# One graph-network layer on one core: staging, counts, first offsets, bias and pads of the setup rearranged

## The reference

```
h   = concat(x[src], x[dst], edge_attr) @ W + b
h   = (h - mean(h)) / sqrt(var(h) + 1e-5) * gamma + beta
out = segment_sum(relu(h), src, 6250)
y   = layernorm(x + out)
```

## Time and profile before

| | us |
|---|---|
| median of 3 runs | 1229.41 |
| profiled execution | 1233.39 |
| its span | 1231.5 |
| TensorE (PE) busy | 986.8 |
| VectorE (DVE) busy | 928.1 |
| POOL busy (784 scatters 766.6) | 782.5 |
| ScalarE (ACT) busy | 711.7 |
| mean granted TensorE clock | 0.947 |

### The profile page before, as it was taken

The page is one execution under the profiler, slowest core; times in us unless marked ns, Lnnn a source line. Parts: engine busy times, 40 slices in busy tenths (PEclk is TensorE's granted clock), DMA queues, the critical chain, the costliest instruction groups (busy, mean ns, idle before and its releaser), DMA issues.

```text
span 1231.5 us, 36181 instructions
## 1 busy us (share of the span) xinstructions
PE 986.8 (80%) x9913; PEld 867.3 (70%) x9914; DVE 928.1 (75%) x2787; ACT 711.7 (58%) x2814; POOL 782.5 (64%) x810
## 2 busy tenths in 40 slices
PE   6789977988888887888787778888887878577784
PEld 5667767887777787777777777777777777566651
DVE  7675447987777777777777777777777777689987
ACT  3324455765655656655555656566556556467765
POOL 0067676777777777777777777777777777700030
PEclk9789888999999989999999999999899999799998
DMA  8677567766666666666766766676666665333303
GB/s 215 180 236 220 175 203 217 239 194 197 195 191 193 191 192 199 199 185 192 194 189 188 199 188 197 188 204 197 192 187 200 194 183 150 113 106 92 99 19 104
DMA packets 192458, 221.57 MB, mean 180 GB/s; under 512 B 51350, under 2 KB 141802, under 8 KB 192272
## 3 DMA queue, kind: packets, MB, share of 16 engines
q1 hardware_dynamic: 166236, 163.92, 48.5%
q0 software_dynamic: 25088, 54.64, 12.0%
q10 hardware_dynamic: 948, 0.79, 0.3%
HBM read 147.95 MB, written 71.30 MB: 178 GB/s over the span
## 4 chain that ended last, share of the span: by engine, by line
DMA 19%; issue 16%; POOL 16%; DVE 16%; PE 15%; ACT 12%; DVEq 3%; SPq 3%; POOLq 0%; ACTq 0%
POOL rows L685 16%; DMA rows<-p,pos_idx 15%; ACT late L1189 6%; DVE late L1586 5%; PE bank L964 3%; DVE room L1570 3%; DVEq L495 2%; ACT turn L1151 2%; PE bank L918 2%; PE bank L858 2%; PE bank L942 1%; DMA tabB<-room 1%; DVE room L1562 1%; PE bank L871 1%; PE bank L869 1%
## 5 line engine op out<-in xcount | busy, mean ns | idle before, releaser
L685 POOL DMA_INDIRECT rows<-p,pos_idx x784 | 766.6, 978 | 309.8 <-issue 275.4
L1189 ACT ACTIVATE late<-room 128x128 f32<-128x128 f32 x864 | 256.1, 298 | 288.7 <-DVE room L1570 286.0
L964 PE MATMUL bank<-wc,turn 128*128 128x128 f32 x1552 | 238.8, 301 | 10.6 <-ACT turn L1151 7.0
L1586 DVE SCALAR_TENSOR_TENSOR late<-room,late,floor 128x128 f32<-128x128 f32 x864 | 245.8, 347 | 0.4 <-issue 0.3
L964 PEld LDWEIGHTS bank<-wc,turn 128*128 128x128 f32 x1552 | 203.6, 205 | 29.4 <-ACT turn L1151 26.0
L918 PE MATMUL bank<-late 128*128 128x129 f32 x1472 | 204.8, 282 | 19.9 <-DVE late L1586 19.7
L918 PEld LDWEIGHTS bank<-late 128*128 128x128 f32 x1472 | 182.7, 194 | 27.8 <-DVE late L1586 25.3
L942 PE MATMUL bank<-room 128*128 x2592 | 201.9, 226 | 0.0
L1181 ACT COPY room<-bank 128x512 bf16<-128x512 bf16 x216 | 126.8, 587 | 100.6 <-PE bank L932 95.5
L1562 DVE TENSOR_TENSOR room<-room,bank 128x129 f32 x432 | 123.8, 287 | 74.3 <-issue 51.3
L942 PEld LDWEIGHTS bank<-room 128*128 128x128 bf16 x2592 | 170.0, 102 | 5.0
(11 more groups left out here) (241 smaller groups left out, 1221.4 us busy)
## 6 DMA issues: line engine op xcount, KB each, us to landing
p<-in_edge_attr_dram SPq DMA_DIRECT2D x98, 512.0 KB
room<-rows SPq DMA_DIRECT2D x256, 136.0 KB
near_bc<-near SPq DMA_DIRECT2D x98, 256.0 KB
late<-rows SPq DMA_DIRECT2D x176, 136.0 KB
rows<-p,pos_idx POOLq DMA_INDIRECT x784
win<-tabB SPq DMA_DIRECT2D x196, 31.5 KB
rows<-fill SPq DMA_DIRECT2D x24, 204.0 KB
tabB<-room SPq DMA_DIRECT2D x12, 384.0 KB, 3.2
```

Source lines behind the costliest of these rows:

```text
L685: nc.gpsimd.indirect_dma_start(rows_ap, bass.IndirectOffsetOnAxis(pos_idx[:, k, j:j + 1], 0), stage[:, k, j, :], None).then_inc(st_free[k] ...
L964: pe.matmul(bank[H_BANK + h][:, t * D:(t + 1) * D], eT[h][:, t * P:(t + 1) * P], wc[:, 2, :], start=(t == 0), stop=False, skip_group_check ...
L1189: a = nc.scalar.activation(junk[b2][:, j, :], pre[b2][:, j, :], ACT.Square, accum_out=ssq[:, b2, j:j + 1])
L1586: a = nc.vector.scalar_tensor_tensor(msg_room[:, b2, j, 0:D], pre[b2][:, j, :], rstd[:, b2, j:j + 1], floor[:], ALU.mult, ALU.max)
```

## The change

- `b_st` has 13 slots, one for each quarter; the wait of `b_high` for a store is gone.
- On TensorE `x_turn(1)` and `b_mult(0)` stand ahead of the turn of the `src` indices; `count_digits` and the product that spreads the counts (now both in bank 3) stand behind the whole table, behind the register load. The product of the starts and `ranks(0)` stand inside the first group, behind its first edge turn.
- On VectorE the window integers come first, then the repeats, the register load, the counts, the one-hot of group 0, then the starts.
- On SyncE the near loads of groups 0 to 2 and the six offset loads stand ahead of the waits for the stores, and a wait for the block totals (`s_tot`) stands ahead of the steps.
- The bias is split into three bf16 parts on three partitions, and its product is [3 rows of ones] by [3 parts]. The split costs VectorE eight more operations; all of it stands after half step 5.
- Even pads stay four a step (25 of them in steps 1 to 7); odd pads come one a step in steps 14 to 37.

```
+        ones_bf = sb("ones_bf", [3, P], BF16)
+        bc_parts = sb("bc_parts", [3, D], BF16)
...
-        b_st = room[:, B_ROOM:B_ROOM + 24 * D]...rearrange(..., k=4, t=4, v=3)
+        b_st = room[:, B_ROOM:B_ROOM + 6 * D * NQ]...rearrange(..., k=NQ, t=4, v=3)
@@ sync
-                load_near(0, 0)
+                for k in range(AHEAD):
+                    load_near(k, k)
+                first_at = [[window_at(k, h) for h in range(2)] for k in range(AHEAD)]
                 for k in range(4):
                     sp.wait_ge(s_tab[k], 16 * (NQ // 4 + (k < NQ % 4)))
-                load_window(0, 0)
-                for k in range(1, AHEAD):
-                    load_near(k, k)
-                    load_window(k, k)
+                for k in range(AHEAD):
+                    for h in range(2):
+                        load_half(k, h, first_at[k][h])
+
+                sp.wait_ge(s_tot, 1)
...
                     if g >= 1:
-                        for bk in pads[4 * g - 4:4 * g]:
-                            fill_pad(bk)
+                        for i in range(4 * g - 4, min(4 * g, EVEN)):
+                            fill_pad(2 * i)
+                    if ODD_AT <= g < ODD_AT + NB - EVEN:
+                        fill_pad(2 * (g - ODD_AT) + 1)
@@ tensor
             x_turn(0)
+            x_turn(1)
+            pe.wait_ge(s_wc, 1)
+            b_mult(0)
             pe.wait_ge(s_idx_f, 1)
             turn_indices(0, (2, 3)).then_inc(s_idx_t, 1)
-            for q in range(NQ):
+            for q in range(1, NQ):
...
-                if q == 8:
-                    count_digits()
                 if q == 10:
-                    pe.wait_ge(s_spread, 1)
-                    pe.matmul(bank[3][:, 0:DU * DV], ones_f[0:DM, :], spread...).then_inc(s_tot, 1)
                     pe.wait_ge(s_win, 1)
...
+            pe.wait_ge(s_wi, 1)
+            wide = groups_without_window(pe)
+            count_digits()
+            pe.wait_ge(s_spread, 1)
+            pe.matmul(bank[3][:, 0:DU * DV], ones_f[0:DM, :], spread...).then_inc(s_tot, 1)
             pe.wait_ge(s_blo, NQ)
-            pe.wait_ge(s_base, 1)
-            pe.wait_ge(s_wi, 1)
-            pe.matmul(ranks_early, ones_f[0:1, :], start[0:1, :], start=True, stop=False, ...)
+            def first_starts():
+                pe.wait_ge(s_base, 1)
+                pe.matmul(ranks_early, ones_f[0:1, :], start[0:1, :], start=True, stop=False, ...)
...
-                pe.matmul(bank[A_BANK + q % 2]..., ones_f[0:1, :],
-                          bc[0:1, :].unsqueeze(1).to_broadcast([1, n, D]), ...).then_inc(s_am, 1)
+                pe.matmul(bank[A_BANK + q % 2]..., ones_bf[:],
+                          bc_parts[:].unsqueeze(1).to_broadcast([3, n, D]), ...).then_inc(s_am, 1)
...
                 def first_edges(h):
                     turn_edges(0, 0, 0, h)
+                    if h == 0:
+                        first_starts()
+                        ranks(0, 0)
...
-                ranks(0, 0)
@@ scalar, b_high
-                if q >= 4:
-                    act.wait_ge(s_tab[q % 4], 16 * (q // 4))
@@ vector
-            (the three operations from the counts to `spread`, ahead of x_copy(10))
...
+            dve.wait_ge(s_wbc, 1)
+            (w_i, w_i[2*NG]: s_wi)
             link(nc.vector.memset(dup[:], 0.0))
             repeats(0, FIRST_REPEATS)
+            dve.wait_ge(s_wi, 1)
+            wide = groups_without_window(dve)
+            (counts to `spread`)
+            block_onehot(0, 0, iota_blk[:])
             dve.wait_ge(s_tot, 1)
             (room_of, end_at, base, start, pad_i)
-            (w_i, w_i[2*NG]: s_wi)
-            block_onehot(0, 0, iota_blk[:])
             block_onehot(1, 1, iota_blk[:])
+            def bias_parts():
+                (b_mean, b_mean / D, bc as before)
+                nc.vector.memset(ones_bf[:], 1.0)
+                whole, rest, least = bc[0:3, :], gain[0:3, :], lift[0:3, :]
+                part = floor[0:3, :].bitcast(BF16)[:, 0:D]
+                link(nc.vector.tensor_copy(part, whole))
+                link(nc.vector.tensor_tensor(rest, whole, part, ALU.subtract))
+                link(nc.vector.tensor_copy(part, rest))
+                link(nc.vector.tensor_tensor(least, rest, part, ALU.subtract))
+                link(nc.vector.tensor_scalar(rest, rest, ident[0:3, 1:2], None, ALU.mult))
+                link(nc.vector.scalar_tensor_tensor(rest, whole, ident[0:3, 0:1], rest, ALU.mult, ALU.add))
+                nc.vector.scalar_tensor_tensor(bc_parts[:], least, ident[0:3, 2:3], rest, ALU.mult, ALU.add).then_inc(s_bias, 1)
...
+                        if t == 5:
+                            bias_parts()
```

More of the change, by code:

```diff
@@ L536, in fill_pad @@
                              fill[:].to_broadcast([P, n // P, PITCH])).then_inc(s_fill if bk % 2 else s_fill0, 16)
-            pads = [bk for bk in range(NB) if bk % 2 == 0] + [bk for bk in range(NB) if bk % 2]
             EVEN = (NB + 1) // 2
+            ODD_AT = 14
+            assert (EVEN + 3) // 4 < FIRST_FULL + 2 and ODD_AT + NB - EVEN <= NG
             regs = [sp.alloc_register(f"sp_off{v}") for v in range(2)]
@@ L755, in b_minus_high @@
                 pe.wait_ge(s_bhi, q + 1)
-                pe.matmul(bank[B_BANK[q % 4]][:, 0:n * D], minus_bf[:], b_st[:, q % 4, 0:n, 0, :], start=False, stop=False,
+                pe.matmul(bank[B_BANK[q % 4]][:, 0:n * D], minus_bf[:], b_st[:, q, 0:n, 0, :], start=False, stop=False,
                           skip_group_check=True).then_inc(s_br, 1)
@@ L761, in b_minus_mid @@
                 pe.wait_ge(s_bmid, q + 1)
-                pe.matmul(bank[B_BANK[q % 4]][:, 0:n * D], minus_bf[:], b_st[:, q % 4, 0:n, 1, :], start=False, stop=True,
+                pe.matmul(bank[B_BANK[q % 4]][:, 0:n * D], minus_bf[:], b_st[:, q, 0:n, 1, :], start=False, stop=True,
                           skip_group_check=True).then_inc(s_brr, 1)
@@ L823, in _ @@
             b_minus_mid(NQ - 1)
+            pe.wait_ge(s_wi, 1)
+            wide = groups_without_window(pe)
+            count_digits()
+            pe.wait_ge(s_spread, 1)
+            pe.matmul(bank[3][:, 0:DU * DV], ones_f[0:DM, :], spread.rearrange("p u v -> p (u v)"), start=True, stop=True).then_inc(s_tot, 1)
             pe.wait_ge(s_blo, NQ)
-            pe.wait_ge(s_base, 1)
-            pe.wait_ge(s_wi, 1)
-            pe.matmul(ranks_early, ones_f[0:1, :], start[0:1, :], start=True, stop=False, skip_group_check=True)
+            def first_starts():
+                pe.wait_ge(s_base, 1)
+                pe.matmul(ranks_early, ones_f[0:1, :], start[0:1, :], start=True, stop=False, skip_group_check=True)
             def ranks(g, k):
@@ L949, in select_a @@
                     select_tile(s, c, at, jj)
[L951 removed]
+            with pe.If_eq(wide, 0):
                 def first_edges(h):
                     turn_edges(0, 0, 0, h)
+                    if h == 0:
+                        first_starts()
+                        ranks(0, 0)
                     pe.wait_ge(eT_ready, h + 1)
@@ L1120, in b_mid @@
                 act.wait_ge(s_br, q + 1)
-                nc.scalar.copy(b_st[:, q % 4, 0:n, 1, :], bank[B_BANK[q % 4]][:, 0:n * D].rearrange("p (t d) -> p t d", t=n)).then_inc(s_bmid, 1)
+                nc.scalar.copy(b_st[:, q, 0:n, 1, :], bank[B_BANK[q % 4]][:, 0:n * D].rearrange("p (t d) -> p t d", t=n)).then_inc(s_bmid, 1)
             def b_low(q):
@@ L1125, in b_low @@
                 act.wait_ge(s_brr, q + 1)
-                nc.scalar.copy(b_st[:, q % 4, 0:n, 2, :], bank[B_BANK[q % 4]][:, 0:n * D].rearrange("p (t d) -> p t d", t=n)).then_inc(s_blo, 1)
+                nc.scalar.copy(b_st[:, q, 0:n, 2, :], bank[B_BANK[q % 4]][:, 0:n * D].rearrange("p (t d) -> p t d", t=n)).then_inc(s_blo, 1)
             for q in range(NQ):
@@ L1400, in _ @@
             nc.vector.tensor_tensor(w_i[0:1, 2 * NG:2 * NG + 1], w_i[0:1, 2 * NG:2 * NG + 1], bank[2][0:1, 2 * NG + 129:2 * NG + 130], ALU.add).then_inc(s_wi, 1)
+            link(nc.vector.memset(dup[:], 0.0))
+            repeats(0, FIRST_REPEATS)
+            dve.wait_ge(s_wi, 1)
+            wide = groups_without_window(dve)
+            dve.wait_ge(s_dcnt, 1)
+            link(nc.vector.tensor_tensor(diagonal, bank[3][0:DM, 0:DV * DC].rearrange("p (v c) -> p v c", v=DV),
+                                         same_col.unsqueeze(1).to_broadcast([DM, DV, DC]), ALU.mult))
+            link(nc.vector.tensor_reduce(col_counts, diagonal, AX.X, ALU.add))
+            nc.vector.tensor_tensor(spread, u_step.unsqueeze(2).to_broadcast([DM, DU, DV]),
+                                    col_counts.unsqueeze(1).to_broadcast([DM, DU, DV]), ALU.mult).then_inc(s_spread, 1)
             def block_onehot(g, k, numbers):
@@ L1598, in _ @@
             after_setup = chain[0]
-            dve.wait_ge(s_wi, 1)
-            with dve.If_eq(groups_without_window(dve), 0):
+            with dve.If_eq(wide, 0):
```

58 lines of the change are left out of this document (27 added, 31 removed).

## The result

The changed kernel takes 1218.35 us (median of 4 runs, 1216.95 to 1219.64), the kernel before in the same comparison 1229.36 (4 runs, 1228.46 to 1231.73): a ratio of 0.9907, 95% interval 0.9890 to 0.9925, 11.0 us less. The profiled execution took 1216.95 us with a span of 1215.0, 16.4 less than the profiled one of before.

A forecast was written before the change was run, and what follows sets the result against it. POOL's scatters bound the kernel, with TensorE pacing groups 3 to 8 and SyncE late in groups 9 to 12. Setup 2.5 + product 8.0 - split 0.6 + pads 3.8 = 13.7 us, so 1215.7 us, range 1209.5 to 1222.5.

The forecast's parts named there:

- likeliest case: Whole kernel: the forecast itself, 1211 to 1218 us, chance 0.58.
- The ramp and what follows it: POOL's scatters: 16.4 us lost before group 13, then 10.25 us a group without idle, so earlier gains last.
- Setup, 2.5: Staging for the whole table with counts behind it: first scatter 2.5 us earlier, from -1.5 to 4.9.
- Windows against products: First group: windows land at 51.7, ahead of TensorE at 52.7; span of 50.3 to 56.7, so they may decide.
- rival 1: Setup gives nearly nothing, by half clock or late windows: gain 11.2 or 9.7 us, 1218 to 1220; chance 0.20.
- Offsets read early, 0: SyncE in the setup: reading six offsets ahead of the store waits gives nothing alone.
- The bf16 product, 8.0: TensorE, half steps 7 to 15: nine bias products each 0.84 us shorter, 8.0 us at granted clock 0.93.
- Rival 3: Bias product: bf16 costs as much as f32, so only 5.7 us gained, 1223.7; chance 0.07.
- The split, -0.6: VectorE after half step 5: eight more operations delay the copy before the column sums by near 0.6 us.
- Pads, 3.8: SyncE steps 7 to 12 lose 24 fills and become near 8 us; groups 8 to 13 gain 3.8 us.
- Rival 5: Slower: odd pads in steps 14 to 37 expose 1.3 us each on SyncE, up to 1247 us; chance 0.04.
- Rival 2: POOL decides from the start and all the ramp goes: 18.9 us gained, 1210.5; chance 0.05.

The follow-up runs named there:

- bias_in_setup: The changed kernel with the split of the bias moved from after half step 5 into the setup; 1214.10 us, ratio 0.9874.
- late_offsets: The changed kernel with near loads and offsets of groups 0 to 2 read where they were before, each ahead of its window; 1217.08 us, ratio 0.9891.
- counts_inside: bias_in_setup with the digit counts back inside the table (q = 8) and their spread at q = 10, the 13 slots kept; 1214.63 us, ratio 0.9892.
- bias_in_setup_f32: bias_in_setup with the bias product again the f32 one of one row; 1223.07 us, ratio 0.9937.
- setup_alone: The kernel before with only the 13 slots, counts behind the table and early offsets; bias and pads as before; 1228.00 us, ratio 0.9965.
- split_in_setup_late_offsets: The changed kernel with the split of the bias in the setup and the offsets of groups 0 to 2 read as before; 1214.20 us, ratio 0.9884.
- old_pads: The changed kernel with the pads as before, four a step in steps 1 to 13; 1222.34 us, ratio 0.9939.
- bias_alone: The kernel before with only the bias split into three bf16 parts in the setup and the bf16 product; 1229.81 us, ratio 0.9983.

## Why the prediction was right, point by point

1215.7 us was forecast and 1218.35 measured, inside the range and inside the likeliest case. The sum was 13.7 us, the medians differ by 11.0. One term, the split, was too small by 3.5 us; that the total is off by only 2.7 owes something to luck, since the terms for setup and product came out 1.8 and 1.0 us on the other side.

- *The ramp and what follows it* was right. POOL's 680 scatters of the steady part take 868.7 us where they took 871.6, so a gain up to group 13 is kept to the end.
- *Setup, 2.5.* Direction right. Measured 4.3 alone, with an interval of 1.7 to 6.9 that holds the 2.5. The last low part was ready near 40.3 (41.3 forecast), the counts ended at 44.07 (45.2), the starts' product stood at 46.55 (47.8), the first window product at 51.65. The clock was the open point, 1.0 us or 3.3. In this profile it stayed at 1.00 and the gain was 4.6. In bias_in_setup, late_offsets and counts_inside it was half for 6.8, 6.8 and 13.7 us between 41 and 57, and the first scatter came at 55.8, 55.9 and 56.5, a gain of 1.8 to 2.5; in bias_in_setup_f32, half for 10.2, it came at 57.4, a gain of 0.9. In setup_alone it was half for 3.4 us, about the first edge products (2.06 us for eight), the wait for the windows covered most of that, and the scatter came at 53.94. So both a gain near 1.0 and one above 3.3 occur, but each of these is one execution of a slightly different kernel.
- The rule of the Trainium skill, "TensorE: Matmul & The Clock Gate", Part 4, that transposes don't count as activity, would have had the clock fall between the counts and the first scatter. The turns at 45.29 and 48.09 stand among other products here, and in the changed profile it didn't fall; in the other profiles it fell, in some before the first of these turns. So these runs neither bear the rule out nor refute it.
- *Windows against products* (part of rival 1) was right in kind: the windows decided, by 0.72 us. *Offsets read early, 0* was right: late_offsets and split_in_setup_late_offsets. The Trainium skill's floor of 600 ns for a register load ("DMA: Bandwidth & Descriptors", Latency and other measured facts) changed nothing here: six reads in series took 3.7 us (near 45.6 to 49.27), 0.62 each with what lies around them, and the windows could be sent from 49.27, where the sum by rows had 48.6. That stretch would fit the floor; the load of 272 ns in the earlier trace rows doesn't.
- *The bf16 product, 8.0.* Measured 7.8 (ratios) to 9.0 (medians) with the new pads. The product took 0.39 us busy (at 87.58) and 0.33 of the path, between the 0.22 and the 0.39 that were weighed; the granted clock of the stretch, 1.00 against 0.91, fits the rest. Rival 3 (it isn't cheap) is refuted. TensorE doesn't decide up to group 8 any more, POOL does from group 4.
- *The split, -0.6.* This is the mis-sized term. It cost about 4 us. I counted the three us of VectorE as covered by 35 of 75 us busy, and priced the delay of one copy. But the share of a stretch says nothing of the place: the copy stood behind all of it in VectorE's order, TensorE waited 1.92 us for it, and after that wait ran the longest block of the half step at half clock, 2.5 us more, which the sum had no term for. With -4.1 instead of -0.6 and 4.3 and 9.0 for the two others the sum would be 13.0; the 2.0 us from there to the measured 11.0 lie within the intervals of the terms.
- *Pads, 3.8.* Measured 4.0 (old_pads). SyncE's steps became 8.5 to 10.1 us (130.39, 140.52, 148.99, 157.81). Rival 5 is refuted: POOL has no idle piece after group 14 that the odd pads make. What I did not see is that the 8.0 of the bias part were worked out as if SyncE let groups 9 to 13 follow. Alone they are 2. With the setup part in, and with it the earlier start of SyncE's queue, the gain comes out with old pads as with new ones; whether the new pads alone would do isn't shown.
- Rival 2 (POOL decides from the start) was wrong for the change but is nearly what bias_in_setup does: 134.5 us from first scatter to group 13, where POOL's own pace needs 133.3.

What stays open: why the granted clock falls in the setup of some executions, and why the drain takes 1.6 us more here (154.3, also in bias_alone 154.5, against 153.1 in setup_alone).

## What to carry to other kernels

Small work that is put "under cover" has to be placed by the wait it stands in, not by an engine's busy share: three us of VectorE cost 0 to 1.4 us where it waited 3.56 us for TensorE (part of which was its own register load), and 4 us ahead of a copy that TensorE waited for. A saving on the engine that sets the pace is worth only what the next engine in line leaves: ask for each stage how long that engine's own step is. The same bf16 product was worth 8 to 9 us with the other two parts in, and 2 us without them. The best version here is the changed kernel with the split in the setup, 1214.1 us, ratio 0.9874 (0.9854 to 0.9894).

## What was unexpected of the hardware

- Nearly the same setup runs at full or half clock from one profile to the next, and the first scatter moves by 2 to 4 us with how long and where it is at half (53.72 with the clock at 1.00; 53.94 and 54.00 with 3.4 us at half; 55.61, 55.82, 55.90, 57.40 and 56.50 with 6.8, 6.8, 6.8, 10.2 and 13.7). Up to 1.4 us of 55.61 and 57.40 is the split in the setup.
- In three of three profiles a wait of 1.9 to 2.1 us at one place was followed by a block at half clock (5.39 us against 2.86), so it cost more than twice its length; in the seven without the wait the block ran at full clock.
- In one set of runs all kernels took 40% more (1732.43 against 1229 to 1232 us), with TensorE idle up to 1.9 us ahead of single products and no wait for it in the profile, and every part of the change gave 0.3% or less there.
